# Five small products of a state-space and expert kernel: dt in one pass, the router's halves in one tile, `D u` scaled on ScalarE, and three turns as plain transposes

## What is computed

```python
# x_dbl has 16 rows of dt, 16 of B and 16 of C
u = silu(conv(in_proj(context)) + conv_b)
x_dbl = einsum('ke,bel->bkl', x_proj_w, u)
delta = softplus(einsum('er,brl->bel', dt_proj_w, dt_lo) + dt_proj_b)
state = state * exp(d_t * A) + (d_t * u_t) * B_t      # scan over 512 tokens, 16 states a channel
y = sum_n(state * C_t) + D * u
x = x + tanh(g_xattn) * (y * silu(layernorm(x).T)).T
# experts
output = expert(x2, Ws1, Wsg, Ws2)                    # shared, silu(x@w1)*(x@wg) @ w2
gate_logits = x2 @ gate_w + gate_b                    # 512 -> 7
# softmax, top 3 of 7, renormalised; output += expert_e(x2) * w_e, x + tanh(g_ffn) * output
```

## Time and profile before

| | |
|---|---|
| runs | 1408.97 us median of 3 (1408.61 to 1411.01) |
| the profiled execution | 1408.53 us, span 1406.7 us |
| TensorE busy | 1362.3 us, 97% of the span, granted clock 0.993 in the mean |
| VectorE busy | 964.6 us, 69% |
| ScalarE busy | 618.5 us, 44% |
| GpSimd busy | 413.5 us, 29% |
| chain that ended last | TensorE 82%, VectorE 11%, issue 4%, ScalarE 2% |
| waits of TensorE on scans (L552) | 23.0 us in 26 waits |
| DMA | 189 GB/s in the mean |

### The profile page before, as it was taken

The page is one execution under the profiler, slowest core; times in us unless marked ns, Lnnn a source line. Parts: engine busy times, 40 slices in busy tenths (PEclk is TensorE's granted clock), DMA queues, the critical chain, the costliest instruction groups (busy, mean ns, idle before and its releaser), DMA issues.

```text
span 1406.7 us, 18118 instructions
## 1 busy us (share of the span) xinstructions
PE 1362.3 (97%) x6290; PEld 1065.3 (76%) x6290; DVE 964.6 (69%) x1107; ACT 618.5 (44%) x1007; POOL 413.5 (29%) x224
## 2 busy tenths in 40 slices
PE   9888799999999999999999999999999999999999
PEld 4454577777777877888888877888888888888887
DVE  6999856799999764689888765598888732112111
ACT  6887455766556225544543235534543222111111
POOL 0000044788889310123332120133332211111111
PEclk8999999999999999999999999999999999999999
DMA  6344336676667853654565653655665555555552
GB/s 219 108 155 157 135 122 233 253 266 240 227 231 270 284 181 125 199 165 156 187 202 194 256 193 112 205 158 164 196 202 182 200 189 194 194 193 179 179 179 89
DMA packets 90797, 266.38 MB, mean 189 GB/s; under 512 B 11472, under 2 KB 11600, under 8 KB 90336
## 3 DMA queue, kind: packets, MB, share of 16 engines
q1 hardware_dynamic: 85472, 258.39, 53.6%
q10 hardware_dynamic: 5248, 6.96, 1.4%
HBM read 207.39 MB, written 57.93 MB: 189 GB/s over the span
## 4 chain that ended last, share of the span: by engine, by line
PE 82%; DVE 11%; issue 4%; ACT 2%; DMA 0%; ACTq 0%; DVEq 0%; POOL 0%
PE ps_hg L474 24%; PE ps_h L474 21%; PE ps_y L474 16%; PE ps_y L633 8%; DVE st L1180 7%; PE ps_mid L552 6%; DVE y_rows L1186 1%; DVE st L1171 1%; PE ps_mid L522 1%; PE ps_mid L515 1%; PE ps_mid L518 1%; PE ps_mid L474 1%; ACT dA L836 1%; PE ps_h L544 0%; PE ps_y L497 0%
## 5 line engine op out<-in xcount | busy, mean ns | idle before, releaser
L1444 POOL TENSOR_TENSOR h_lo<-h_tmp,h_hi 128x512 fp32r<-128x512 f32 x128 | 256.9, 2007 | 743.9 <-ACT h_hi L913 700.7
L474 PE MATMUL ps_h<-x_hi,w_split 128*128 128x512 f32 x1024 | 345.9, 399 | 1.6 <-DVE x_lo L1239 1.4
L474 PE MATMUL ps_hg<-x_hi,wg_split 128*128 128x512 f32 x1024 | 345.0, 398 | 0.1
L1309 DVE TENSOR_TENSOR h_tmp<-h_tmp,ps_hg 128x512 f32<-128x512 f32 x128 | 88.0, 688 | 318.5 <-PE ps_hg L474 317.5
L1180 DVE TENSOR_TENSOR_SCAN st<-dA,st 128x1024 f32<-128x1024 f32 x128 | 305.8, 2398 | 0.0
L474 PE MATMUL ps_y<-w_split,h_hi 128*128 128x512 f32 x1024 | 258.1, 400 | 0.0
L913 ACT ACTIVATE h_hi<-h_tmp 128x512 fp32r<-128x512 f32 x128 | 80.6, 630 | 350.0 <-DVE h_tmp L1309 350.0
L474 PEld LDWEIGHTS ps_h<-x_hi,w_split 128*128 128x128 f32 x1024 | 192.3, 188 | 42.0 <-DVE x_lo L1239 1.7
L474 PEld LDWEIGHTS ps_hg<-x_hi,wg_split 128*128 128x128 f32 x1024 | 192.3, 188 | 39.8 <-issue 0.5
L474 PEld LDWEIGHTS ps_y<-w_split,h_hi 128*128 128x128 f32 x1024 | 190.3, 190 | 38.5
L907 ACT ACTIVATE h_tmp<-ps_h 128x512 f32<-128x512 f32 x128 | 76.2, 595 | 293.1 <-PE ps_h L474 293.1
(11 more groups left out here) (143 smaller groups left out, 1127.5 us busy)
## 6 DMA issues: line engine op xcount, KB each, us to landing
w_split<-split_scratch SPq DMA_DIRECT2D x192, 512.0 KB, 5.0
wg_split<-split_scratch SPq DMA_DIRECT2D x96, 512.0 KB, 4.2
split_scratch<-w_split SPq DMA_DIRECT2D x64, 512.0 KB, 3.7
b_all<-xd_scratch SPq DMA_DIRECT2D x64, 256.0 KB, 4.1
split_scratch<-wg_split SPq DMA_DIRECT2D x32, 512.0 KB, 3.0
w_raw<-in_W_dram SPq DMA_DIRECT2D x14, 1024.0 KB, 7.1
wg_raw<-in_Wg_dram SPq DMA_DIRECT2D x7, 1024.0 KB, 9.7
dA<-in_x_dram SPq DMA_DIRECT2D x4, 1024.0 KB, 7.8
```

The costliest lines, as they stand in the source:

```text
L474: mm = pe.matmul(out_, lhs[a], rhs[c], start=first and q == 0, stop=last and q == len(sides) - 1)
L1309: dve.tensor_tensor(h_tmp[j % 2][:], h_tmp[j % 2][:], ps_hg[:], ALU.mult).then_inc(h_made, 1)
L1444: pool.tensor_tensor(h_lo[:, j, :], h_tmp[j % 2][:], h_hi[:, j, :].bitcast(F32), ALU.subtract).then_inc(hl_ready, 1)
```

## The change

- **dt:** `x_proj_w` is laid out on the host as 80 rows: dt, B, dt, C, dt. `dt_x` is a float32r copy of all 80, and its third block (rows 32 to 47) is replaced by what rounding took away (`front_dt_low` on VectorE). `dt_w` holds dt's weights in blocks 0 and 2 and the rounding rest in block 4, with zeros beside B and C. One float32r matmul over 80 rows then gives the three products that count. `dt_w` is rounded by ScalarE and its rest made by VectorE in the start-up, and TensorE's first front waits for that.
- **Router:** the high and low halves of `gate_w` lie side by side in one tile `gw` (7 + 7 columns), so two passes for each k are enough. The logits come out as two halves, which VectorE adds (one more instruction in `router`).
- **`D u`:** `scale_u` on ScalarE writes D u to `st[0]` at j = 2 of the shared step, and TensorE turns it by transposes. Batch 0 keeps its matmul with `diag_D`.
- **C columns and logits:** plain transposes of 128x128 of `xdbl`, which now has 128 rows.
- `xd_scratch` holds B only, and the wait for `r_exp` in `router_rows` goes.

```diff
-        gw_hi = sb("gw_hi", [P, T, P], F32R)
-        gw_lo = sb("gw_lo", [P, T, P], F32R)
+        gw = sb("gw", [P, T, P], F32R)
+        halves = sb("halves", [P, T, 2 * NE])
...
-        xdbl = sb("xdbl", [XP, L])
-        logits_T = xdbl[0:NE]
+        xdbl = sb("xdbl", [P, L])
+        logits_T = xdbl[0:2 * NE]
+        dt_raw = y_rows[0:DRP, 0, :]
...
                     elif kind == "init":
                         for et in range(T):
-                            mm = pe.matmul(ps[:, et * P:(et + 1) * P], u[:, et, i * P:(i + 1) * P], diag_D[:, et, :],
-                                           start=True, stop=True)
+                            pe.wait_ge(ud_ready, T * (m - 1) + et + 1)
+                            mm = pe.transpose(ps[:, et * P:(et + 1) * P], st[0][:, et, i * P:(i + 1) * P], ident[:])
                     elif kind == "dt":
-                        pe.wait_ge(*taken(m, front_place(m, "xproj")))
-                        mm = pe.matmul(ps[:], dt_w[:, i * P:(i + 1) * P], xdbl[0:DR, :], start=True, stop=True)
+                        pe.wait_ge(dt_low, m + 1)
+                        mm = pe.matmul(ps[:], dt_w[:, i * P:(i + 1) * P], dt_x[:], start=True, stop=True)
                     elif kind == "ccols":
                         pe.wait_ge(*taken(m, front_place(m, "xproj")))
                         for i in range(T):
-                            mm = pe.matmul(ps[:, i * DS:(i + 1) * DS], xdbl[0:XP, i * P:(i + 1) * P],
-                                           ident[0:XP, XP - DS:XP], start=True, stop=True)
+                            mm = pe.transpose(ps[:, i * P:(i + 1) * P], xdbl[:, i * P:(i + 1) * P], ident[:])
...
-                    mm = three_passes(ps_mid[bank][:], [gw_hi[:, k, :], gw_lo[:, k, :]], [x_hi[:, k, :], x_lo[:, k, :]],
-                                      ((0, 0), (0, 1), (1, 0)), k == 0, k == T - 1)
+                    mm = three_passes(ps_mid[bank][:], [gw[:, k, :]], [x_hi[:, k, :], x_lo[:, k, :]],
+                                      ((0, 0), (0, 1)), k == 0, k == T - 1)
...
-                    mm = pe.matmul(ps_mid[bank][:, i * 8:i * 8 + NE], logits_T[:, i * P:(i + 1) * P], ident[0:NE, 0:NE],
-                                   start=True, stop=True)
+                    mm = pe.transpose(ps_mid[bank][:, i * P:(i + 1) * P], xdbl[:, i * P:(i + 1) * P], ident[:])
...
+            pe.wait_ge(dt_w_low, 1)
             front(0, "xproj", "dt0", "dt1", "dt2", "dt3", "ccols")
...
+            def scale_u(m):
+
+                for et in range(T):
+                    act.wait_ge(u_ready, T * m + et + 1)
+                    act.activation(st[0][:, et, :], u[:, et, :], ACT.Copy, scale=D_col[:, et:et + 1]).then_inc(ud_ready, 1)
...
                 act.wait_ge(mid_done[bank], before + 1)
+                act.activation(dt_x[:], ps_mid[bank][0:XP, :], ACT.Copy).then_inc(dt_high, 1)
                 if some(m):
                     act.wait_ge(xd_st, 16 * m)
-                act.activation(xdbl[:], ps_mid[bank][0:XP, :], ACT.Copy).then_inc(mid_read[bank], 1)
+                act.activation(xdbl[0:XP], ps_mid[bank][0:XP, :], ACT.Copy).then_inc(mid_read[bank], 1)
...
+            def front_dt_low(m):
+
+                rows = slice(2 * DR, 3 * DR)
+                dve.wait_ge(dt_high, m + 1)
+                dve.wait_ge(*taken(m, front_place(m, "xproj")))
+                dve.tensor_tensor(dt_x[rows], xdbl[rows], dt_x[rows].bitcast(F32), ALU.subtract).then_inc(dt_low, 1)
...
+                    link(dve.tensor_tensor(logits[:], halves[:, :, 0:NE], halves[:, :, NE:2 * NE], ALU.add))
...
             first_conv(3)
+            rows = slice(4 * DR, 5 * DR)
+            dve.wait_ge(dt_w_high, 1)
+            dve.tensor_tensor(dt_w[rows], dt_raw[rows], dt_w[rows].bitcast(F32), ALU.subtract).then_inc(dt_w_low, 1)
+            front_dt_low(0)
             front_z_stats(0, range(T))
...
+                    if p == 5:
+                        front_dt_low(m)
```

More of the change, by code:

```diff
@@ L34, in gated_block @@
     DC = t["conv_w"].shape[1]
-    DR = t["dt_wT"].shape[0]
-    XP = DR + 2 * DS
+    DR = t["dt_wT"].shape[0] // 5
+    XP = 5 * DR
+    XC = 3 * DR
+    DRP = XP
     TOP_K = 3
@@ L59, in gated_block @@
         xproj_w = sb("xproj_w", [P, T, XP])
-        dt_w = sb("dt_w", [DR, DI])
+        dt_w = sb("dt_w", [DRP, DI], F32R)
+        dt_x = sb("dt_x", [DRP, L], F32R)
         conv_w = sb("conv_w", [P, T, DC])
@@ L157, in gated_block @@
         dt_read = sem("dt_read")
+        dt_high = sem("dt_high")
+        dt_low = sem("dt_low")
+        dt_w_high = sem("dt_w_high")
+        dt_w_low = sem("dt_w_low")
         e_ready = sem("e_ready")
@@ L479, in keep_warm @@
                 for _ in range(count):
-                    pe.matmul(bank[:], gw_hi[:, 0, :], gw_hi[:].rearrange("p k e -> p (k e)"),
+                    pe.matmul(bank[:], gw[:, 0, :], gw[:].rearrange("p k e -> p (k e)"),
                               start=True, stop=True).then_inc(warm, 1)
@@ L744, in _ @@
                 (xproj_w[:], t["xproj_wT"].rearrange("(t p) c -> p t c", p=P)),
-                (dt_w[:], t["dt_wT"]),
+                (dt_raw, t["dt_wT"]),
                 (D_col[:], t["D"]),
@@ L805, in front_ccols @@
                 act.wait_ge(mid_done[bank], before + 1)
[L806 removed]
+                ps = ps_mid[bank][:].rearrange("p (t n) -> p t n", t=T)[:, :, XC:XC + DS]
                 act.activation(c_cols[:], ps, ACT.Copy).then_inc(mid_read[bank], 1)
@@ L882, in router_columns @@
                 act.wait_ge(xd_st, 16 * (b + 1))
-                act.activation(logits_T[:], ps_mid[bank][0:NE, :], ACT.Copy).then_inc(mid_read[bank], 1)
+                act.activation(logits_T[:], ps_mid[bank][0:2 * NE, :], ACT.Copy).then_inc(mid_read[bank], 1)
             def router_rows(b):
@@ L887, in router_rows @@
                 act.wait_ge(mid_done[bank], before + 1)
[L888 to L891, removed]
+                ps = ps_mid[bank][:].rearrange("p (i e) -> p i e", i=T)[:, :, 0:2 * NE]
+                act.activation(halves[:], ps, ACT.Copy).then_inc(mid_read[bank], 1)
             def split_hi(step, w, name, j):
@@ L932, in between @@
                 def between(j):
+                    if j == 2 and m is not None:
+                        scale_u(m)
                     if j == 3 and m is not None:
@@ L1025, in _ @@
             act.wait_ge(const_ld, 16 * NCONST)
+            act.activation(dt_w[:], dt_raw, ACT.Copy).then_inc(dt_w_high, 1)
             act.activation(gate_tanh[:], gates[:], ACT.Tanh).then_inc(setup_a, 1)
@@ L1242, in router @@
             def router(m, part):
-                links = 12
-                first = 6
+                links = 13
+                first = 7
                 done = [first if part else 0]
@@ L1503, in columns @@
         return v.reshape(-1, P).T
+    dr = g["dt_proj_w"].shape[1]
+    dt, b_rows, c_rows = (g["x_proj_w"][i * dr:(i + 1) * dr] for i in range(3))
+    xproj = np.concatenate([dt, b_rows, dt, c_rows, dt])
+    dt_wT, gap = g["dt_proj_w"].T, np.zeros_like(g["dt_proj_w"].T)
+    dt_wT = np.concatenate([dt_wT, gap, dt_wT, gap, dt_wT])
     arrays = {
         "x": g["x"], "ctxT": g["ctx_1024"].transpose(0, 2, 1), "g_xattn": g["g_xattn"], "g_ffn": g["g_ffn"],
-        "in_wT": g["in_proj_w"].T, "conv_w": g["conv_w"], "conv_b": columns(g["conv_b"]), "xproj_wT": g["x_proj_w"].T,
-        "dt_wT": g["dt_proj_w"].T, "dt_b": columns(g["dt_proj_b"]), "A_log": g["A_log"], "D": columns(g["D"]),
+        "in_wT": g["in_proj_w"].T, "conv_w": g["conv_w"], "conv_b": columns(g["conv_b"]), "xproj_wT": xproj.T,
+        "dt_wT": dt_wT, "dt_b": columns(g["dt_proj_b"]), "A_log": g["A_log"], "D": columns(g["D"]),
         "W1": g["W1"], "Wg": g["Wg"], "W2": g["W2"], "Ws1": g["Ws1"], "Wsg": g["Wsg"], "Ws2": g["Ws2"],
```

15 lines of the change are left out of this document (8 added, 7 removed).

## The result

The changed kernel takes 1390.29 us (median of 4 runs, 1389.26 to 1390.95) where the kernel before, beside it, takes 1408.79 (4 runs, 1407.59 to 1411.01): a ratio of 0.9866, 95% interval 0.9852 to 0.9880. That is 18.5 us off where 23 were forecast. The profiled execution took 1390.95 us with a span of 1389.2.

A forecast was written before the change was run, and what follows sets the result against it. TensorE, busy for 97% of the span, was taken as the bound, with VectorE in the start-up. From 1408.53 us, 28.0 off less 2.1 of waits and 2.9 of start-up gave 23.0 off: 1385.5 us, range 1379 to 1394.

The forecast's parts named there:

- router, with the x product: Shared step: router columns 0.93 us less, rows 0.71 less, each four times; the x product on 80 rows changes nothing.
- dt, less the waits: Shared step: each dt falls from 1.05 to 0.30 us, twelve times, 9.0 us; new bank waits cost 2.1 in all.
- C turn: Shared step, C columns: transposes make the turn and the passes behind it 0.72 us shorter, three times, 2.2 us.
- clock fall gone: Behind the C turn, first two batches: thin work shrinks, so both clock falls go, 2 x 1.60 = 3.2 us.
- 0.59 less, four groups: `D u` in the shared step: 1.09 us becomes 0.50 a group, in each of three batches, 7.1 us.
- the wait for dt1's bank: First batch's shared step: dt2 gets dt1's bank 5.8 us after the gate product's end, a wait of about 0.4.
- dt0 comes one up product later: hidden: Shared step: VectorE's `front_dt_low`, one subtraction of 0.66 us, costs nothing because dt0 comes later.
- hands this on to the end: Start-up: `delta * u` starts at 39.9, and the saturated scans pass on its 2.9 us delay; bounds 0 and 5.
- rival 1: The clock still falls in the first two batches: 1388.7 us, chance 0.15.
- the start-up's delay was not taken up: Start-up: the rival had the scans' later waits absorb VectorE's delay, 1382.6 us, chance 0.08.
- transposes did not keep the clock low: Shared-step fronts: the rival had transposes hold the clock low, 64 us lost, 1449 us, chance 0.03.
- Rival 2: Shared-step front: ScalarE and the two banks set the pace, 2 us more a batch, 1391.5 us, chance 0.12.

The follow-up runs named there:

- experiment 12: The kernel before with the router's halves in one tile and the x product on 80 output rows, nothing else changed: 1397.87 us, ratio 0.9917.
- experiment 5: The changed kernel with dt and the turn of the C columns both as before, router and `D u` as changed: 1392.81 us, ratio 0.9883.
- experiment 3: The changed kernel with only the turn of the C columns as before, by a float32 matmul: 1390.23 us, ratio 0.9864.
- experiment 2: The changed kernel with only `D u` as before, by matmuls with `diag_D` and no scaling on ScalarE: 1392.70 us, ratio 0.9882.
- experiment 7: The kernel of experiment 1 with ScalarE's copy of init1 moved ahead of the exponential and its table load: 1384.39 us, ratio 0.9822.
- experiment 6: The kernel before with 28 instead of 20 filler matmuls ahead of the first expert step: 1404.89 us in one run, beside a median of 1409.84.
- experiment 4: The changed kernel with only dt as before, a float32 matmul over 16 rows with no split and no start-up wait: 1391.60 us, ratio 0.9875.
- experiment 1: The changed kernel with TensorE's wait for dt_w's low part behind the x product and both low-part subtractions after z's statistics: 1385.98 us, ratio 0.9832.
- experiment 8: The kernel of experiment 7 with 35 instead of 20 filler matmuls ahead of the turns of x2: 1384.77 us, ratio 0.9824.
- experiment 9: The kernel before, unchanged, profiled once more: 1410.05 us in one run.
- experiment 10: The changed kernel with 28 instead of 20 filler matmuls in the start-up: 1388.97 us, ratio 0.9853.
- experiment 11: The kernel before with 24 instead of 20 filler matmuls in the start-up: 1410.01 us, ratio 1.0003.

## Why the prediction was right, and where it was not

The direction and the place were right, and so was the bound: what was taken off TensorE in batches 2 to 4 came off the time, but for the part that the wait at the C turn covered. Laid out from experiments 12, 5, 3 and the changed kernel, the second batch's step goes 52.64, 51.04 without the fall, 49.11, 47.13, 44.13, 43.66:

| term, per batch | forecast | measured |
|---|---|---|
| router, with the x product | 1.64 + 0 | 1.93 |
| `D u` | 2.36 | 1.98 |
| dt, less the waits | 3.0 - 0.4 | 3.00 |
| C turn | 0.72 | 0.47 |
| clock fall gone | 1.60 | 1.60 |

The total (8.9 forecast, 9.0 measured) is better than its parts: the router's row and dt's are 0.3 and 0.4 above the forecast, `D u` and the C turn 0.4 and 0.25 below. That they cancel is in part luck, in part that the forecast booked a shared price under the wrong edit.

- **Router.** Right: 1.63 in the last batch, where nothing else changes.
- **x product, "nothing".** Too low by some 0.3 a batch. It lost 0.13, and the 0.2 by which the first `D u` group behind it was dearer went too. The forecast booked that 0.2 under `D u`, so it moves from one row to the other.
- **`D u`.** The price of 0.59 was right nowhere. Beside the old dt a group is worth 0.5 (experiment 12 against 5), as the transposes are then dearer too (0.59 for 0.44). With the new dt it is 0.45, and the last of the edits to be put in finds part of its gain under a wait (experiment 2: 1.3 where the sum had 2.36). The step "0.59 less, four groups" took the kernel before as the surroundings of each edit; the edits share the cost of changing over and may claim it once only.
- **dt.** A pass over 80 rows takes 0.23, the floor; 0.30 was the pessimistic side, worth 0.9 us in all. The wait at the C turn took 0.8 (experiment 7) where 0.4 stood for the later batches. In one batch, four dt at 0.82 less and three groups behind them at 0.14 less, which the forecast had under `D u`, give 3.7, less 0.8 for the wait 2.9; 3.00 was measured.
- **C turn.** 0.47 for 0.72. The turn went from 1.07 to 0.66 and the 16 passes behind it from 3.74 to 3.67. The forecast had 0.50 and 3.63 for the two; what is missing is the 0.22 by which a turn behind a wait is dearer (0.44 without it, experiment 7). In the first batch the C turn was worth nothing.
- **The first batch.** With the fall on its first product set aside, experiments 6, 12, 5 and 3 and the changed kernel give: router and x product 1.90, `D u` 1.99, dt less the waits 1.56 (1.7 forecast), C turn 0, fall 1.60. That is 7.0 where 8.0 stood. From the end of the fourth gate product to dt2 the chain is not on TensorE in the changed kernel, but on VectorE's normalisation and router and ScalarE behind them:

```profile
209.21 0.69 DVE h_tmp L1333
209.90 1.83 DVE dA L1136 x4
...
212.65 0.61 ACT h_hi L926
...
214.36 0.58 ACT delta L831
```

  It takes 5.9 us, with dt or the C turn as before as well (experiments 3, 4 and 5), so in this batch dt1 and the C turn gave nothing in that stretch. The forecast had its length right (5.8), as the wait for dt1's bank.
- **The waits of the first batch.** Two of them stood in the forecast. In all, TensorE waited 0.54 us for `dt_x`, 0.42 for init1, 0.47 for dt1 and 0.16 for `h_hi`: 1.6 where 1.3 stood, and the pass behind such a wait is dearer (dt 0.48 for 0.23, a turn 0.66 for 0.44). The step that failed is "dt0 comes one up product later: hidden": that wait and the dearer pass behind it cost 0.8 us, of the size of what the step lacks (1.0). The timeline of the changed kernel, ScalarE, GpSimd, VectorE and TensorE:

```profile
199.05 2.55 ACT L799 ACTIVATE st<-u,D_col 128x512 f32<-128x512 f32 x4
...
202.54 0.58 ACT L812 ACTIVATE dt_x<-ps_mid 80x512 fp32r<-80x512 f32 x1
...
203.45 1.29 POOL L1480 TENSOR_TENSOR wg_split<-wg_raw,wg_split 128x512 fp32r<-128x512 f32 x1
...
203.70 1.58 DVE L1153 TENSOR_TENSOR dt_x<-xdbl,dt_x 16x512 fp32r<-16x512 f32 x1 [3.84 <-ACT xdbl L815]
...
205.43 0.48 PE L531 MATMUL ps_mid<-dt_x,dt_w 80*128 80x512 f32 x1 [0.54 <-DVE dt_x L1153]
```

  and of the kernel with `D u` as it was (experiment 2), which has no `scale_u`:

```profile
200.46 0.59 ACT L812 ACTIVATE dt_x<-ps_mid 80x512 fp32r<-80x512 f32 x1 [1.20 <-PE ps_mid L524]
...
200.86 1.28 POOL L1472 TENSOR_TENSOR h_lo<-h_tmp,h_hi 128x512 fp32r<-128x512 f32 x1
...
201.64 1.05 DVE L1151 TENSOR_TENSOR dt_x<-xdbl,dt_x 16x512 fp32r<-16x512 f32 x1 [3.05 <-ACT xdbl L815]
...
202.10 1.74 POOL L1478 TENSOR_TENSOR wg_split<-wg_raw,wg_split 128x512 fp32r<-128x512 f32 x1
...
203.90 0.39 PE L531 MATMUL ps_mid<-dt_x,dt_w 80*128 80x512 f32 x1
```

  Behind `scale_u` the copy comes 1 us after the x product's end at 201.5 (0.2 after it without), and dt0 waits; without, it doesn't. My list of what is queued behind `scale_u` had `h_hi`, its split and `front_xd`, and I did not follow the `dt_x` copy, which is in `front_xd`, to dt0. VectorE's subtraction, taken at 0.66, is 1.58: it ends 0.54 us after the GpSimd instruction that was running when it started, and 0.55 after it in experiment 2, where that one ended sooner. dt as before (experiment 4) tells what that cost: once the fall on the first product is set aside (1.56 us in the changed kernel, none on it in experiment 4), dt is worth 1.5 us in this batch and 3.0 in the two others.
- **Start-up.** The mechanism was right, the size was not: 2.9 forecast, 5.0 between the changed kernel and experiment 1 (177.66 to 172.62). The 39.9 of the text was 40.49, as VectorE's subtraction started at 24.77, when the forecast had it end. But "hands this on to the end" left no room for the two places where VectorE then waits for others who are late too: 1.27 and 1.02. The delay at the last scan was 5.86 in this profile, above the bound of 5, and 3.8 to 4.1 in the three other kernels with the wait; the term of 2.9 was too small by 1 to 3 us. Not all of it is the wait: in experiment 1, which keeps the new dt without it, `delta * u` is 0.7 us earlier than before and the last scan still 0.6 later.
- **Where the table's first two rows blur.** Before, the first fall lies on the transposes of x2 (1.97 and 1.62 us for two groups of eight, one of which takes 0.87 in the earlier trace rows), ahead of the first product; after, it lies on the product (4.60 for 3.04). So the start shows 4.74 and not 5.86, and the first shared step a gain of 5.45 and not 7.0. Against the forecast the start is 3.0 worse, and the step 1.0 (the waits and what is dearer behind them); the rest is the fall's dearer place, 0.4, and the routed steps.
- **Routed steps.** Forecast unchanged, 0.7 longer in the first batch: TensorE waited 0.83 for `h_tmp` (L1333). A small thing with no experiment of its own.
- **The clock.** The amount came as forecast and the reason isn't shown, so that term came right by luck as far as the runs tell. Experiment 5 has dt and C as before and no fall. Experiment 8 has neither and a fall. Experiment 6 is the kernel before without any. What the fourteen profiles say together is this: where the router's part and the x product of 80 rows are in, 1 of 30 shared steps has a fall behind its fronts; without them, it is 7 of 12 (2, 2, 3 and 0 in the four profiles). Three of those four profiles have falls within a microsecond of 209 and 537 us, and with 8 fillers some 40 us ahead of the first of them both are gone. So the moment at which work arrives may have a part in it, and what the kernel before runs in its shared steps another: all seven have, and all thirty lack, the x product on 48 output rows, the router's third pass and its logits turned by narrow matmuls. None of these was put back by itself, executions differ among themselves in the mean clock (experiments 9 to 11), and this stays open. Of the gain of 18.5 us, 3.2 are thus a matter of where falls land, and a small edit elsewhere can give them back. The Trainium skill ("TensorE: Matmul & The Clock Gate", Part 4: PE-mode transpose) says that a transpose in transpose mode does not count as busy for TensorE in the same way. No run here shows a cost of it: in the changed kernel's shared steps the groups of transposes stand between products and the clock beside them is 1.00. The one fall behind such a group is that of experiment 8.

The rivals: no fall is left behind the C turns in the profile of the changed kernel (rival 1), the start-up's delay was not taken up, the routed steps kept their pace but for 0.7 us, and transposes did not keep the clock low. Rival 2, ScalarE with two banks setting the front's pace, is what the first batch and the C turn show in small: 0.8 us where 0.4 was booked in each later batch, and it vanishes there when the copy is moved (experiment 7).

## What to carry to other kernels

Price edits that stand side by side in one sum, with the last one's surroundings and not those of the kernel before: a change-over between kinds of product, or a wait, can only be saved once. A wait put ahead of a full engine in the start-up costs what its later waits don't take up (3.4 us of 4.9 here), and what it then waits for others that are late too, so look for work in its queue that doesn't depend on it and put that first (here 4.3 us for a move of two instructions and a wait). And take a bank's copy ahead of a table load when TensorE wants the bank; it gave 0.8 us where TensorE was next on the chain, and nothing in the first batch, where VectorE and ScalarE were.

## What the runs showed of the hardware

- Behind a product that fills 16 rows, four transposes take 0.58 us where they take 0.44 behind one of 80 or 128; a float32 `D u` group takes 1.09 where it takes 0.89. The x product on 48 output rows did the same to its follower, and took 3.56 instead of 3.43 itself.
- A float32r pass of 512 columns over 80 rows takes 0.23 us, one of float32 over 16 rows 0.52 with its change-over.
- VectorE's subtraction on 16 partitions takes 0.68 us alone (835.56 in the changed kernel). With a GpSimd instruction on other tiles under way when it starts, it ends 0.54 or 0.55 us after that one: it takes 1.58 us in the changed kernel and in experiments 1, 3, 7, 8 and 10, and 1.05 in experiment 2. The GpSimd instruction that began beside it in experiment 2 took 1.74 instead of 1.3. That fits the one waiting for the other, which no run isolates.
- The kernel before has its two falls in the shared steps within a microsecond of the same place in three profiles, one of them with four more fillers; eight more took both away. Unprofiled executions of one kernel differ by up to 0.005 in the mean granted clock (0.989 to 0.994 in experiment 11), so one profile does not tell how often a fall comes.
